# A one-core graph and attention kernel: the end of the attention rearranged, and each gather of node rows held until a number of one-hot blocks is made

## The reference

```
x = x + conv(_gn(x))                 # gated scans along both axes of the image, layer norm, projection
t = tokens(x)
t = t + attention(_ln_t(t))          # 16 heads of 4 channels, 256 tokens per image
t = t + ffn(_ln_t(t), edge_index)    # what follows
```

```
h = (x_flat @ W_gat).reshape(M, HEADS, NUM_EXPERTS)      # 4 heads x 4
a_src = (h * att_src).sum(-1); a_dst = (h * att_dst).sum(-1)
e = leaky_relu(a_src[src] + a_dst[dst], 0.2)             # one per edge, 262144 edges and one loop per node
ee = exp(e - segment_max(e, dst)[dst])
alpha = ee / segment_sum(ee, dst)[dst]
agg = segment_sum(h[src] * alpha, dst)
gates = softmax over the two best of mean over heads of layernorm(agg)
out = sum over experts of gate * (gelu(x @ W1[e] + b1[e]) @ W2[e] + b2[e])
```

## Time and profile before

| what | value |
|---|---|
| median of 3 runs | 1069.02 us (1068.75 to 1070.32) |
| profiled execution | 1070.63 us |
| its span, first to last instruction | 1069.1 us |
| busy TensorE | 618.4 us, 58% |
| busy VectorE | 706.2 us, 66% |
| busy ScalarE | 413.3 us, 39% |
| busy GpSimd | 320.4 us, 30% |
| mean granted TensorE clock | 0.752 of full |

### The profile page before, as it was taken

The page is one execution under the profiler, slowest core; times in us unless marked ns, Lnnn a source line. Parts: engine busy times, 40 slices in busy tenths (PEclk is TensorE's granted clock), DMA queues, the critical chain, the costliest instruction groups (busy, mean ns, idle before and its releaser), DMA issues.

```text
span 1069.1 us, 12844 instructions
## 1 busy us (share of the span) xinstructions
PE 618.4 (58%) x4608; PEld 306.5 (29%) x4608; DVE 706.2 (66%) x1462; ACT 413.3 (39%) x727; POOL 320.4 (30%) x384
## 2 busy tenths in 40 slices
PE   1505623698888888889886312012017999795412
PEld 1201210243344434433344200001003444344411
DVE  3799885975888888878768100001016988888975
ACT  3613510252555555535445700100105778542015
POOL 1000000084667767200000777777740000000000
PEclk8758765585999999978887655555557999899555
DMA  5000031000000000000011411110110000000001
GB/s 154 0 0 39 16 82 37 1 2 1 1 2 1 0 0 0 0 1 1 1 59 36 84 10 10 10 10 9 10 6 1 1 1 1 1 1 1 3 2 40
DMA packets 21993, 16.93 MB, mean 16 GB/s; under 512 B 13488, under 2 KB 18944, under 8 KB 21168
## 3 DMA queue, kind: packets, MB, share of 16 engines
q1 hardware_dynamic: 15424, 14.02, 4.8%
q0 software_dynamic: 5392, 2.18, 2.5%
q10 hardware_dynamic: 1120, 0.00, 0.1%
HBM read 10.51 MB, written 2.54 MB: 12 GB/s over the span
## 4 chain that ended last, share of the span: by engine, by line
DVE 37%; PE 28%; another core or an unknown queue 13%; issue 7%; ACT 5%; SPq 2%; DMA 0%; DVEq 0%; ACTq 0%
DVE mx L1358 9%; DVE arena L1438 8%; PE psum L611 8%; PE psum L762 5%; PE psum L666 3%; PE psum L627 3%; PE psum L642 2%; SPq L406 2%; DVE arena L1094 2%; DVE arena L1090 2%; ACT arena L1064 1%; ACT arena L982 1%; DVE mz L1377 1%; PE psum L741 1%
## 5 line engine op out<-in xcount | busy, mean ns | idle before, releaser
L1438 DVE TENSOR_TENSOR arena<-arena,psum 128x4096 bf16<-128x4096 bf16 x64 | 143.2, 2284 | 210.1 <-remote 139.8
L1358 DVE TENSOR_REDUCE mx<-psum 128x2 f32<-128x512 f32 x256 | 164.3, 684 | 62.5 <-PE psum L627 61.2
L954 ACT ACTIVATE arena<-psum 128x1024 f32<-128x1024 f32 x128 | 130.9, 1023 | 118.2 <-PE psum L642 118.2
L496 POOL DMA_INDIRECT work<-node_rows,idx x160 | 152.7, 954 | 53.1 <-issue 48.4
L762 PE MATMUL psum<-arena 128*128 128x512 bf16 x256 | 69.6, 424 | 154.8 <-DVE arena L1438 111.4
L611 PE MATMUL psum<-arena 128*32 128x256 f32 x1024 | 153.5, 426 | 1.0 <-ACT arena L962 0.5
L473 POOL TENSOR_SCALAR work<-arena,cF 128x184 f32<-128x184 f32 x128 | 93.3, 741 | 117.7 <-DVE arena L1232 60.0
L627 PE MATMUL psum<-arena 32*128 32x256 bf16 x512 | 82.9, 305 | 31.5 <-DVE mx L1358 19.5
L1007 ACT COPY arena<-psum 128x256 f32<-128x256 f32 x32 | 11.6, 364 | 224.5 <-remote 127.5
L762 PEld LDWEIGHTS psum<-arena 128*128 128x128 bf16 x256 | 25.5, 106 | 194.1 <-DVE arena L1438 118.7
L611 PEld LDWEIGHTS psum<-arena 128*32 128x32 f32 x1024 | 52.4, 117 | 64.2 <-issue 36.6
(11 more groups left out here) (314 smaller groups left out, 960.4 us busy)
## 6 DMA issues: line engine op xcount, KB each, us to landing
work<-work SPq DMA_DIRECT2D x48, 64.0 KB, 2.0
work<-node_rows,idx POOLq DMA_INDIRECT x160
arena<-in_L_ffn_edge_index_dram SPq DMA_DIRECT2D x2, 1024.0 KB, 13.0
work<-edge_nodes SPq DMA_DIRECT2D x4, 368.0 KB
digits<-arena SPq DMA_DIRECT2D x1, 1024.0 KB, 3.9
arena<-digits SPq DMA_DIRECT2D x1, 1024.0 KB, 5.9
arena<-in_jpat_dram SPq DMA_DIRECT2D x1, 1024.0 KB, 7.6
out_dram<-work SPq DMA_DIRECT2D x4, 256.0 KB, 2.3
```

The source lines that it names most:

```text
L496: pool.indirect_dma_start(gath[:, l, :], None, tab, bass.IndirectOffsetOnAxis(ap=idx[:, l:l + 1], axis=0)).then_inc(done, 16)
L954: act.activation(pbuf[:, n % 4, :, :, :], ps[:, 2 + 2 * (n % 2):4 + 2 * (n % 2), :].rearrange("p j (k q) -> p j k q", k=U), ACT.Exp).then_ ...
L1358: v.reduce_max(mx[:, h, :], ps[:, h % 2, :].rearrange("p (u k) -> p u k", u=U), AX.X).then_inc(mx_done, 1)
L1438: v.tensor_tensor(oh[:, buf, 0:HB, :], jp, pdig[:, here].rearrange("p (j c) -> p j c", j=1).broadcast_to([P, HB, HC]), ALU.is_equal).then_ ...
```

## The change

It has three parts.

1. *Slots.* `slots_end` runs two asides earlier (at n = 85 in place of 87). Finished outputs are transposed early by `turn_finished`: images 0 to 3 ahead of the last `turn_outputs`, 4 to 11 behind it, the last four when all are normalised; VectorE copies chunk 0 ahead of its last `normalise` and does three sort rounds more before it, one more before the residual, four in the norm.
2. *Node rows.* `wpair`, 128 by 48, holds `wext` of both parities on its diagonal, so that one product makes both parities' rows; the results are copied and stored in two halves of eight column blocks. A logarithm that nobody reads stands ahead of each layer norm on ScalarE. `idx` has a semaphore of its own, `rows_listed`, which comes before the rest of `finish_lists`.
3. *Gathers.* Gather l waits until 2l/5 - 7 one-hot blocks are made, where that is over zero (from l = 20 on).

```diff
+        wpair = part2(13264, 2 * NF)
@@ SyncE
-            sp.wait_ge(hb_done, 2)
-            sp.dma_start(tab..., hbt...).then_inc(tab_stored, 16)
-            sp.wait_ge(tab_stored, 16)
+            for k in range(2):
+                sp.wait_ge(hb_done, k + 1)
+                sp.dma_start(tab...[:, 8 * k:8 * k + 8, :], hbt...[:, 8 * k:8 * k + 8, :]).then_inc(tab_stored, 16)
+            sp.wait_ge(tab_stored, 32)
@@ GpSimd
                 for l in range(first, last):
+                    if l < USUAL and 2 * l // 5 - 7 > 0:
+                        pool.wait_ge(h_ready, 2 * l // 5 - 7)
                     pool.indirect_dma_start(gath[:, l, :], ...).then_inc(done, 16)
-            pool.wait_ge(idx_ready, 1)
-            pool.wait_ge(tab_stored, 16)
+            pool.wait_ge(rows_listed, 1)
+            pool.wait_ge(tab_stored, 32)
@@ TensorE
+            def turn_finished(first, last):
+                for b in range(first, last):
+                    mm = pe.transpose(lo[:, b * P:(b + 1) * P], o[:, b, :, :]..., ident)
+                    if b % 4 == 3:
+                        mm.then_inc(s_ot, 1)
                     if m == 4 and later(i, 1):
+                        if not one and not two:
+                            turn_finished(0, 4)
                         turn_outputs(i - 2, three)
+            pe.wait_ge(exp_done, 8 * B)
+            turn_finished(4, B - 4)
             pe.wait_ge(o_done, B)
-            for b in range(B):
-                (the 16 transposes)
+            turn_finished(B - 4, B)
-            pe.wait_ge(wext_done, 1)
+            pe.wait_ge(wext_done, 2)
             for c in range(NCH):
                 pe.wait_ge(ln_out, NCH + c + 1)
                 for b in range(4 * c, 4 * c + 4):
-                    for u in range(U):
-                        mm = pe.matmul(ps[:, u, b * NF:(b + 1) * NF], tn[C * u:C * u + C, ...], wext[C * u:C * u + C, :], ...)
-            mm.then_inc(hb_ready, 1)
+                    mm = pe.matmul(ps[:, b // 8, ...], tn[:, b * P:(b + 1) * P], wpair, ...)
+                if c % 2:
+                    mm.then_inc(hb_ready, 1)
@@ ScalarE
             def layernorm(k):
+                act.activation(bcol[:, UNREAD:UNREAD + 1], bcol[:, EPSC:EPSC + 1], ACT.Ln)
-            act.wait_ge(hb_ready, 1)
-            for u in range(U):
-                act.copy(hbt[:, :, u, :], ps[:, u, 0:B * NF]...).then_inc(hb_done, 1)
+            for k in range(2):
+                act.wait_ge(hb_ready, k + 1)
+                act.copy(hbt[:, 8 * k:8 * k + 8, :, :]..., ps[:, k, 0:8 * U * NF]).then_inc(hb_done, 1)
@@ VectorE
-                    elif n == 8 * (B - 5) - 1:
+                    elif n == 8 * (B - 5) - 3:
                         slots_end()
+                g.link(v.memset(wpair, 0.0))
+                for u in range(U):
+                    v.tensor_copy(wpair[C * u:C * u + C, u * NF:(u + 1) * NF], wext[C * u:C * u + C, :]).then_inc(wext_done, 1)
-                g.step(v.tensor_scalar(idx[:], idt, ...))
+                v.tensor_scalar(idx[:], idt, ...).then_inc(rows_listed, 1)
+                v.wait_ge(rows_listed, 1)
-            sort_bucket(9, 14)
+            sort_bucket(9, 17)
+            v.wait_ge(s_ot, 1)
+            v.tensor_copy(xc[:, cs(0)], ps[:, 0, :]).then_inc(s_ote[0], 1)
             normalise(B - 1)
-            for c in (0, 2):
-                v.wait_ge(s_ot, c + 1)
-                v.tensor_copy(xc[:, cs(c)], ps[:, c, :]).then_inc(s_ote[0], 1)
+            v.wait_ge(s_ot, 3)
+            v.tensor_copy(xc[:, cs(2)], ps[:, 2, :]).then_inc(s_ote[0], 1)
+            sort_bucket(17, 18)
-            layernorm(2, tn, ..., lambda: sort_bucket(14, 18))
-            sort_bucket(18, CAP // 8)
+            layernorm(2, tn, ..., lambda: sort_bucket(18, 22))
+            sort_bucket(22, CAP // 8)
```

More of the change, by code:

```diff
@@ L124, in build @@
         BI, BG, BL, GA, BE, BO, BP = range(7)
-        NBL, EPSC, DIGC, LASTC = 7, 8, 9, 10
+        NBL, EPSC, DIGC, LASTC, UNREAD = 7, 8, 9, 10, 11
         bqk = sb("bqk", [P, 1])
@@ L311, in build @@
         wext_done = sem("wext_done")
+        rows_listed = sem("list_rows_ready")
         class Steps:
@@ L410, in _ @@
             sp.dma_start(part2(8192, 2048, U16), jpat).then_inc(jp_loaded, 16)
-            sp.wait_ge(hb_done, 2)
-            sp.dma_start(tab.rearrange("(b n u) f -> n b (u f)", n=NP_, u=U), hbt.rearrange("p b u f -> p b (u f)")).then_inc(tab_stored, 16)
-            sp.wait_ge(tab_stored, 16)
+            for k in range(2):
+                sp.wait_ge(hb_done, k + 1)
+                sp.dma_start(tab.rearrange("(b n u) f -> n b (u f)", n=NP_, u=U)[:, 8 * k:8 * k + 8, :],
+                             hbt.rearrange("p b u f -> p b (u f)")[:, 8 * k:8 * k + 8, :]).then_inc(tab_stored, 16)
+            sp.wait_ge(tab_stored, 32)
             for q in range(4):
@@ L667, in turn_outputs @@
                 mm.then_inc(ot_ready, 1)
+            def turn_finished(first, last):
+                for b in range(first, last):
+                    mm = pe.transpose(lo[:, b * P:(b + 1) * P], o[:, b, :, :].rearrange("p u c -> p (u c)"), ident)
+                    if b % 4 == 3:
+                        mm.then_inc(s_ot, 1)
             def body(i, buf, one, two, three):
@@ L704, in _ @@
             batches(pe, body, turn_slots)
+            pe.wait_ge(exp_done, 8 * B)
+            turn_finished(4, B - 4)
             pe.wait_ge(o_done, B)
-            for b in range(B):
-                mm = pe.transpose(lo[:, b * P:(b + 1) * P], o[:, b, :, :].rearrange("p u c -> p (u c)"), ident)
-                if b % 4 == 3:
-                    mm.then_inc(s_ot, 1)
+            turn_finished(B - 4, B)
             for c in range(NCH):
@@ L718, in _ @@
                 for b in range(4 * c, 4 * c + 4):
-                    for u in range(U):
-                        mm = pe.matmul(ps[:, u, b * NF:(b + 1) * NF], tn[C * u:C * u + C, b * P:(b + 1) * P],
-                                       wext[C * u:C * u + C, :], start=True, stop=True)
-            mm.then_inc(hb_ready, 1)
+                    mm = pe.matmul(ps[:, b // 8, b % 8 * U * NF:(b % 8 + 1) * U * NF], tn[:, b * P:(b + 1) * P], wpair, start=True, stop=True)
+                if c % 2:
+                    mm.then_inc(hb_ready, 1)
             pe.wait_ge(idx_ready, 1)
@@ L972, in _ @@
             layernorm(2)
-            act.wait_ge(hb_ready, 1)
-            for u in range(U):
-                act.copy(hbt[:, :, u, :], ps[:, u, 0:B * NF].rearrange("p (b f) -> p b f", b=B)).then_inc(hb_done, 1)
+            for k in range(2):
+                act.wait_ge(hb_ready, k + 1)
+                act.copy(hbt[:, 8 * k:8 * k + 8, :, :].rearrange("p b u f -> p (b u f)"), ps[:, k, 0:8 * U * NF]).then_inc(hb_done, 1)
             def low_steps(half, first):
@@ L1264, in fold_scores @@
                     g.link(v.tensor_tensor(attt[:, n, :], wext[:, 0:GF], attb[:, n, :], ALU.mult))
[L1265 to L1269, removed]
+                    g.step(v.reduce_sum(wext[:, GF + 4 * n:GF + 4 * n + 4], attt[:, n, :].rearrange("p (h e) -> p h e", h=4), AX.X))
+                g.link(v.memset(wpair, 0.0))
+                for u in range(U):
+                    v.tensor_copy(wpair[C * u:C * u + C, u * NF:(u + 1) * NF], wext[C * u:C * u + C, :]).then_inc(wext_done, 1)
             def aside(i, m):
@@ L1308, in finish_lists @@
                 g.link(v.tensor_copy(idt, keys[:]))
-                g.step(v.tensor_scalar(idx[:], idt, T - 1, T - 1, ALU.bitwise_xor, ALU.bitwise_and))
+                v.tensor_scalar(idx[:], idt, T - 1, T - 1, ALU.bitwise_xor, ALU.bitwise_and).then_inc(rows_listed, 1)
+                v.wait_ge(rows_listed, 1)
                 g.link(v.tensor_single_scalar(idt, idt, 12, ALU.logical_shift_right))
@@ L1425, in _ @@
                 v.scalar_tensor_tensor(x1[:, cs(c)], ps[:, c, :], bcol[:, BP:BP + 1], x1[:, cs(c)], ALU.add, ALU.add).then_inc(ln_in, 1)
-            layernorm(2, tn, lambda c, ins: ins.then_inc(ln_out, 1), lambda: sort_bucket(14, 18))
-            sort_bucket(18, CAP // 8)
+            layernorm(2, tn, lambda c, ins: ins.then_inc(ln_out, 1), lambda: sort_bucket(18, 22))
+            sort_bucket(22, CAP // 8)
             finish_lists()
```

## The result

| what | before | after |
|---|---|---|
| median (four runs each) | 1069.44 us (1068.75 to 1070.32) | 950.82 us (948.48 to 955.78) |
| profiled execution, span | 1070.63, 1069.1 us | 955.78, 954.2 us |
| stage of the 64 one-hot blocks | 597.40 to 966.84: 369.4 us | 594.24 to 851.83: 257.6 us |
| behind it | 102.3 us | 102.4 us |

The ratio is 0.8896 [0.8869, 0.8923]. 976 was forecast, 925 to 1040 for the forecast's own case. In the profiled execution 115 us go; the stage alone gives 112 of them.

A forecast was written before the change was run, and what follows sets the result against it. TensorE's finished instructions reach other engines at one per 1.40 us while gathers flow. Small terms give 10.6 us; first block 586.8, stall to 712, 57 blocks at 2.85 to 874, then 102.3: 976 us, range 900 to 1045.

The forecast's parts named there:

- the forecast's own case: Whole kernel: the stall drains after 100 to 150 us, or blocks go at up to 5 us; 925 to 1040, chance 0.66.
- How long until it drains?: One-hot block stage: 7800 packets at 53 per us take 148 us; 135 taken, to 712, with seven blocks made.
- The other reading: Flow, in the one-hot stage: each gather occupies the path 1.40 us; half overlapped 5.0 us per block, total 1009.
- The serial rival: One-hot stage: gather and block one after the other, 3.5 + 2.75 = 6.25 us per block, total 1089; chance 0.10.
- The stall never builds up: Start of the one-hot stage: 20 to 25 free gathers are too few for a stall; 870 to 925, chance 0.14.
- VectorE holds the gathers: One-hot stage: gathers wait for VectorE's blocks, 1.25 + 2.29 us each, 140 take 496 us; over 1150, chance 0.02.
- Table loads: Layer norms: an unread Ln moves a 1.28 us load earlier; gain 1.0 third norm, 0.95 second, 1.9 in sum.
- Slots: Attention: the instructions ending the slots run two asides earlier, so TensorE's turn starts sooner; gain 2.1 us (1 to 2.9).
- Finished outputs: Attention's end: twelve of 16 transposes move ahead of the last normalisation, projection starts earlier; gain 2.1 us (0.5 to 3).
- Node rows: Behind the norm: 32 matmuls instead of 64, last normalised chunk to last copy 1.5 us, not 6.25; gain 4.8 (3 to 5).
- fold_scores: Added setup work: a memset and two small copies, under 0.4 us; cost 0.3 us.
- The tail: Behind the last one-hot block: 102.3 us, untouched; a risk if TensorE's reports are still slow there.

## Why the prediction was right, and where it was not

*Place and sign* were right: the waits bring 108 of 119 us, by ending the stall of TensorE's reports. That the gathers then end shortly before the blocks was forecast too, though they end 21 us before them (830.4, 851.8) and not 4 (870, 874).

*The size of the stage* was forecast as 287 us (586.8 to 874) and measured 257.6. The step that failed is "How long until it drains?": it let a backlog of 7800 packets drain at 53 per us, 148 us by that sum and 135 as taken, and then put no stall beside the blocks. Of SyncE's packets 4160 more changed nothing. What drained was gathers alone, 25 of them at 1.40 us: 4 us behind the 25th the path was free, and blocks 8 and 9 were made by 640, not at 710 to 730. In exchange the stall came back behind each clump of gathers, so that blocks went at 3.80 us and not 2.85. The two errors have opposite signs. Up to the start of block 10 the stage took 55.7 us (594.24 to 649.90) and not 125.2 for seven blocks and 8.6 for three; the 54 blocks from there took 201.9 and not 153.9. That is 78 less and 48 more, 30 in all.

*The other reading* was the right one, and the bound that the prediction drew from it, 5.0 us per block with gather and block half overlapped, was too high. 2.5 gathers at 1.40 are 3.5 us, blocks are 2.75, and 3.80 is near the larger: they overlap almost wholly. That VectorE and TensorE run ahead while no gather is out would explain it; no run tests that apart. The serial rival (6.25 per block) falls by the same number.

*"The stall never builds up"* named 870 to 925. It did build up, but an even pace reaches that range (900.66). The change can't reach it: its 160 gathers take as long as at an even 1.55 us (583.8 to 830.4), a pace that costs no block anything, but inside a clump they go at 1.25, which is what stalls.

*VectorE holds the gathers*: not over the one-hot blocks, beside which a gather is 0.94 us. But the gather at 628.93 took 3.05 us beside VectorE's L1340 (628.88, 2.28 us, float32, both inputs in SBUF). That agrees with the Trainium skill (SBUF — State Buffer, Who interferes with whom) for two SBUF inputs beside a reading GpSimd. In the changed kernel only three gathers took over 1.2 us, and they cost the stage nothing that shows.

*The small terms.* Table loads: 1.0 in the third norm as forecast, 0.5 in the second, not 0.95. Slots: 1.4 us between the two profiled executions (from the eleventh turn of outputs to the last one, 106.5 and 105.0), not 2.1; but that stretch takes 106.5 to 108.4 us in the other traces without the earlier slots and 102.9 to 107.6 in those with them, so the size stays open. Finished outputs: 4.2, not 2.1; the forecast counted the projection's start but not that its inputs would come soon enough for 3.60 us back to back. Of the 4.2 the change gave at least 3.1: from the last turn of outputs to the projection's end it is 7.0 us in every trace with the change, and without it 11.2 in two and 10.1 in four. Node rows: 0.4, not 4.8. The failed step is "8 matmuls at 0.11 (0.9)": a matmul of the full product takes 0.22 us, TensorE is behind the norm's last chunk by 5 us in both kernels, and nothing moved. The store in two halves gave the gathers 1.2 us that the forecast had no term for. The terms' sum is 7.5 (with fold_scores below what shows) for the first block and 8.7 for the first gather, and the first gather came 4.3 us sooner, the first block 3.2: some 4 were lost in the attention's loop, which took 381.5 us in place of 378.6, its gain by the slots included. One of its images took 25.4 us at a granted clock of 0.73, its neighbours 20.5 at 1.00; the slowest such image of the trace before took 23.1 at 0.81. In four of the eight traces of kernels with the changed attention the first gather is at 574.8 to 577.2, beside the forecast 577.5, in the other four at 583.8 to 589.5. By medians the two parts are worth 11 (ratio 0.9894), the 10.6 forecast, but by other terms than forecast: that the sums agree is luck.

*The tail*, 102.3 us forecast, was 102.4: the last gather's issue ended at 831.3, 20 us before the last count began (851.89), and no report was late there.

*What stays open.* Which path a finished TensorE instruction and a gather share. The runs say that a gather takes 1.40 us of it whatever its rows, and that TensorE's instructions get through at one per 1.40 us while gathers come 1.21 to 1.25 us apart. Why it is one per 0.6 to 0.9 us at 1.36, where the path is taken just as fully by the sum above, no run shows. Each timed execution here has a span and a granted clock, so each was recorded by the profiler; no run shows whether the recording itself has a part in it. Also open is whether 1.40 goes by the gather or by its packets, whose number half the rows did not change.

## What to carry to other kernels

When a wait on a TensorE count ends as "remote" or "issue" while GpSimd issues indirect transfers back to back, divide the waits by the instructions between two counts: a constant quotient (1.40 us here) says that reports get out at a fixed rate. It does not say whether a backlog or the flow sets that rate; the prediction had the quotient and chose the wrong one. A run with the transfers evenly spaced tells them apart. Here the cure was to space them just above the quotient (1.46 us: 900.66) rather than to tie them to progress, which let them out in clumps (950.82). Spacing costs nothing as long as the last transfer isn't what the end waits for, so look for the pace at which both just end. And before a half-height product is merged into a full one, divide its row's time by its count: at 0.11 us each, half of the full product's 0.22, merging gains nothing.

## What the hardware showed that was not expected

- TensorE's instructions are reported one per 1.40 us while gathers come 1.21 to 1.25 us apart, with 128 rows or 64. At 1.36 and 1.42 us apart the reports are late in part, and at 1.46 and 1.50 us no one-hot block waits for them.
- The stall ends 224 us after the first of 160 unheld gathers (224.2 to 224.6 us in five traces with gathers 1.21 to 1.25 us apart), 1.40 us for each.
- At 1.2 GHz, 64 matmuls of 64 rows by 24 columns took 7.02 us and 32 of 128 rows by 48 columns 7.03.
- A gather's issue, 0.94 us, took 3.05 us beside a VectorE instruction of 2.28 us with two SBUF inputs.
